# Matrix products that nobody reads, in spare PSUM banks, and newly made engine orders, in a two-layer sequence model on one Trainium2 core

## What is computed

```python
xn = layernorm(x)
# block 1: delta-rule attention (4 heads, dk 128, dv 32) plus two layers of
# local attention (8 heads of 64, window 64) with a gelu feed-forward each
x = x + delta_attention(xn) + local_ffn_depth_2(xn)
xn = layernorm(x)
# block 2: causal attention over a latent of 32 (16 heads of 8)
# plus a mixture of 6 experts (top 2) and one shared expert
x = x + latent_attention(xn) + moe(xn)
```

## Time and profile before

| | |
|---|---|
| time, median of 3 runs | 2025.28 us (2022.1 to 2027.91) |
| the profiled execution's own time | 2022.87 us |
| its span, first to last instruction | 2021.0 us |
| PE busy | 1769.2 us (88%) |
| DVE / ACT / POOL busy | 1351.1 / 927.8 / 818.0 us |
| mean granted TensorE clock | 0.941 |

### The profile page before, as it was taken

One profiled execution on the slowest core, in us unless ns is written; L12 is line 12 of the kernel. 1 busy time (PEld: TensorE's weight loads), 2 busy tenths in 40 slices (PEclk: granted clock), 3 DMA queues, 4 the chain that ended last, 5 costly groups with the idle time before them and its releaser, 6 DMA issues.

```text
span 2021.0 us, 43924 instructions
## 1 busy us (share of the span) xinstructions
PE 1769.2 (88%) x16640; PEld 1142.2 (57%) x16640; DVE 1351.1 (67%) x3602; ACT 927.8 (46%) x2449; POOL 818.0 (40%) x819
## 2 busy tenths in 40 slices
PE   2598669999898989999898989999899989988687
PEld 1375437656584647756575646746475556745343
DVE  3454637777678767787687776687587776575273
ACT  1233425366433745357443754446443754435323
POOL 2344635265145534166144534176144544163000
PEclk9789879999899989999899999999899998999788
DMA  4200112100222012200221012110221011220020
GB/s 177 67 26 12 39 33 62 49 20 23 53 57 58 11 37 77 64 21 12 64 57 49 20 35 71 52 38 10 63 62 49 20 36 31 61 65 4 6 80 6
DMA packets 126625, 89.91 MB, mean 44 GB/s; under 512 B 42168, under 2 KB 113976, under 8 KB 126136
## 3 DMA queue, kind: packets, MB, share of 16 engines
q1 hardware_dynamic: 126128, 86.44, 16.0%
q10 hardware_dynamic: 288, 0.67, 0.1%
HBM read 46.84 MB, written 25.17 MB: 36 GB/s over the span
## 4 chain that ended last, share of the span: by engine, by line
PE 67%; DVE 12%; ACT 8%; issue 6%; POOL 6%; DMA 1%; SPq 0%; DVEq 0%; POOLq 0%; ACTq 0%
PE bank L688 10%; PE bank L1076 4%; PE bank L718 3%; PE bank L795 3%; ACT shared L1322 3%; PE bank L1062 3%; PE bank L775 3%; PE bank L805 3%; PE bank L829 2%; PE bank L1061 2%; PE bank L834 2%; ACT soft L1236 2%; PE bank L1153 2%; PE bank L1034 2%; PE bank L961 2%
## 5 line engine op out<-in xcount | busy, mean ns | idle before, releaser
L1322 ACT ACTIVATE shared<-bank 128x512 f32<-128x512 f32 (+1 forms) x384 | 201.8, 531 | 257.7 <-PE bank L1062 256.4
L1818 POOL TENSOR_TENSOR soft<-soft,prec 128x512 f32<-128x512 f32 x128 | 132.6, 1039 | 441.9 <-DVE prec L1457 441.1
L1626 DVE TENSOR_REDUCE nmx<-bank 128x1 f32<-128x512 f32 (+3 forms) x352 | 223.3, 638 | 98.6 <-PE bank L1034 95.6
L1236 ACT ACTIVATE soft<-bank,nmax 128x128 f32<-128x128 f32 x512 | 179.8, 381 | 121.0 <-DVE nmax L1449 120.3
L1779 POOL TENSOR_TENSOR qk_rs<-qk_rs,minus_half 128x16 f32<-128x16 f32 x64 | 187.5, 2930 | 5.3
L1061 PE MATMUL bank<-b_sb 128*128 128x128 bf16 x512 | 116.8, 229 | 39.7 <-ACT shared L1322 38.6
L1062 PE MATMUL bank<-shared 75*128 75x384 bf16 (+3 forms) x512 | 147.1, 315 | 0.0
L718 PE MATMUL bank<-w_sb,hT 128*128 128x512 f32 x256 | 137.9, 628 | 9.1 <-DVE hT L1396 4.7
L1034 PE MATMUL bank<-shared 72*128 72x256 bf16 (+3 forms) x512 | 126.8, 300 | 0.0
L688 PE MATMUL bank<-c_sb,soft 128*128 128x128 f32 x608 | 99.6, 293 | 25.1 <-POOL soft L1818 14.3
L1076 PE MATMUL bank<-shared,vaug 128*32 128x512 f32 (+3 forms) x1024 | 99.7, 489 | 18.9 <-ACT shared L1322 18.1
(11 more groups left out here) (247 smaller groups left out, 4532.5 us busy)
## 6 DMA issues: line engine op xcount, KB each, us to landing
shared<-parts_dram SPq DMA_DIRECT2D x64, 288.0 KB
vm<-v_f SPq DMA_DIRECT2D x112, 128.0 KB, 2.4
parts_dram<-parts SPq DMA_DIRECT2D x96, 128.0 KB, 2.4
L_dram<-the SPq DMA_DIRECT2D x32, 256.0 KB, 2.4
shared<-X_dram SPq DMA_DIRECT2D x32, 256.0 KB, 3.5
shared<-L_dram SPq DMA_DIRECT2D x32, 256.0 KB, 4.1
w_sb<-weights SPq DMA_DIRECT2D x1, 4167.0 KB, 19.2
x_tm<-x SPq DMA_DIRECT2D x8, 256.0 KB, 3.4
```

The source lines that it names most:

```text
L1236: a = af(v4(p_sb, 2, 4)[:, j, g], place("fS", j)[:, g * P:(g + 1) * P], ACT.Exp, bias=nmax[:, at:at + 1], accum_out=psums[:, at:at + 1])
L1322: af(v4(PTm, 2, GROUP)[:, u % 2, i, 0:n], place("mST", b, i)[:, 0:n], ACT.Exp).then_inc(mexp_done, 1)
L1626: reduce(v3(nmx[:], HM)[:, h:h + len(heads), c], v3(place("mS", b, t)[:, 0:len(heads) * (c + 1) * P], len(heads)), AX, ALU.max, negate=Tru ...
L1818: tt(p, p, spread(prec[:, at:at + NPAIR], P), ALU.mult).then_inc(fnorm_done, 1)
```

## The change

**1. Products that nobody reads.** A step `warm` on PE issues 8 products of the bf16 identity by 128x512 bf16 columns into a bank that is unused at that time. There are 19 such steps, 152 products: 7 in period -1 (behind `hT`, each `fv` and each `k`), 4 in the first layer of period 0 and 4 in its second (each behind an `fS`), and 4 that may stand anywhere ahead of the first `mST` of period 8. The four of the first layer wait for the last `gram` (bank 3), those of the second for `oT0` (bank 0), the last four for the last `fkT` (bank 5). The first `k` of batch 1, which uses bank 3 again, waits for `warm_done`.

**2. All orders anew.** All strings of all five engines and all periods differ, those of periods 1 to 6 and 7 too, in which there is no `warm` step.

```diff
 ORDER = {
     "PE": (
         (
-         "fefeffeefeffefefeeeeee"),
...
+         "feeefeefeefeeffeffeeefeefeffe"),
...
+WARM = 8
...
-            s += [("fS", b, l, c)] + [("fnorm", b, l, c, j) for j in range(2)]
+            s += [("fS", b, l, c)] + ([("warm", "l0" if l == 0 else "l1", WARM)] if b == 0 else []) + [("fnorm", b, l, c, j) for j in range(2)]
...
-    s = []
+    s = [("warm", "end", WARM)] * 4 if b == LAST else []
...
+def warmed(steps, names):
+
+    return [x for step in steps for x in [step] + ([("warm", "start", WARM)] if step[0] in names else [])]
...
-        first = {"f": steps_head(0) + [("hcopy", 0)] + steps_chunks(0, 0, 0, AHEAD), "e": steps_early(0)}
+        first = {"f": warmed(steps_head(0) + [("hcopy", 0)] + steps_chunks(0, 0, 0, AHEAD), ("hT", "fv")), "e": warmed(steps_early(0), ("k",))}
...
+        BANKS = {"warm": lambda site: {"start": 2, "l0": 3, "l1": 0, "end": 5}[site],
...
+                def idle(site, n):
+
+                    if site == "l0":
+                        pe.wait_ge(L_done, NT)
+                    elif site == "l1":
+                        pe.wait_ge(oT0_copied, 1)
+                    elif site == "end":
+                        pe.wait_ge(fkT_copied, ch(BATCH, 0, 0))
+                    for _ in range(n):
+                        m = mm(v3(place("warm", site)[:], 4), B("identb"), repeat(B("identb"), 4), start=True, stop=True, skip_group_check=True)
+                    if site == "l0":
+                        m.then_inc(warm_done, 1)
...
                         if b:
                             pe.wait_ge(oT0_copied, b)
+                        if b == 1:
+                            pe.wait_ge(warm_done, NT)
```

More of the change, by code:

```diff
@@ new lines @@
+         "beffebbbfbffefbefbeebbebebffebfebfbbffbbfbbfffbfbbbbfbbbbbbbbbb"),
+        (
+         "bdmffdbdmdbdfbmddbddffdbddfmdfdbbdbmdbddfmddfdfdbdddmbdbmbddbdfddedfdmddmbddmdddbdbdbdbdmdbddmdbdmbbbbdbbambma"
+         "fafamdfafamfafafafmabamfafabbmbacacfcabcmaccfafcamacbcfacamcabcfbacmcbcafcbacfmcafcabcamccfaeacbbaecabcaecacec"
+         "afbceacbcafccaefaecabebcaefceccaeacbcaeabceccabcafcfccfbcccbccfbbcbccfbccbccbccbccccbc"),
+        (
+         "bdmdffbdbdmbfdmbdfddfddbdfdmfdbdbdbdmbddddfmdffmbdmffdbbdbdbdbdddmbdbmdbdbdmdbddddbdbbbbdbbddbdmmfddddmdfdmdff"
+         "fmafmaadmamfamfafabafmambafmabfabmabmaffacbacmcfacmfabccabcfabcabcfaccabccaffcaacbbccabcaabcabcaccaabcabcabcab"
+         "accbacccacacbcacbcabbababacbabcacbccacccbccccccccccccccccccccccc"),
@@ L67 @@
-        (
-         "bdffdbbddmbdmdddffffdbbfbfbmdmdddfmmmfddbfdbbbddfddddbbmddbbmdddbddfdmfffffmfffmfbbdbcbcffccmffccbcfbcbcbcffcf"
-         "ccbcffcbbcbcccbccbcbcbccccccccbccccccccccccccccccccbcc"),
+         "fdddddfbbbbfddfdddfbdfbbbfffdfddbdfbbddfdbdddbdbdbdbbdddffdddfffdffefefebeebfbbffffeebefebbbfffbffbbffbfffbbbb"
+         "fbffb"),
+        (
+         "bddfbdbfdmdfbdmdddffbfdbddbfbffdfmddbmmbmbdmbdddffdbmdbbbdddddddmdbdffdfmfffffbfmbbcfcbccfcffccmcbcfcbfcbccbfc"
+         "fcfcmcbcfecbbeccbececfccecbecfecfecebcfcbccbcccfccfcccfccbccccfcfcccccb"),
@@ L70 @@
+        (
+         "bfdddbdbfbmdmfdfdfbdfdbfdbdbffddfmmmmbffmdbbdbdbdddbdbddbdmbfddddmdfddffffmfmffdbfbmbbffffccmcbcfbcbcbcffcfccc"
+         "bcfbcbcbcfccbcbcbcbcccccccccbccccccccccccbcccccccccccc"),
         (
-         "mmmmmmmmmmmmccccccccmccccccccccccccccccccccccccccccccccccccccccccc"),),
+         "mmmmmmmmmmmmmccccccccccccccccccccccccccccccccccccccccccccccccccccc"),),
     "DVE": (
         (
-         "ffffeffeeeffeeeeee"),
+         "fffffeeeefefeefeee"),
         (
-         "bddfbbfddefbddbdbdfdbddddddeddbdbddbbddddbddbdddbdbdddddbbddbbddbeddbbbbdfffefeeebbbffebfbbfbeefebebbbfebfbbbf"
@@ new lines @@
+         "bbbbbbbbbbbb"),
+        (
+         "bbmbefmfdddmmmdbmddmbddbmbdfddedbmddfdddmbdmdbbdmmddmdddbddmddmbdbdbddddddmbbmdbdedbmbmbdbdabmbamafafamafafama"
+         "mabababmafaamafambaaambababmafamaffacabambmababaaaeeaeaaebababceabaaffaeaeaaeabbeabafbfbcebbbbbcbc"),
+        (
+         "bmbbfmfmdmddmdbmddbdmbdmbdfddfbdddddmdmmbbmbmdddbbdmbdbmddmddbbddbddbdbddbmdbdbdbdmmfddddmfdmfmafamamamaamafba"
+         "bmamabfamamaabmafbambabafaaabaambaabbaaaabacbababaaaabbabaababacaaabababbababccc"),
@@ L98 @@
         (
-         "feefeefee"),
+         "fefefeeee"),
         (
-         "eddffddfffeefeeefef"),
+         "deddffdfffeeeeeefff"),
         (
-         "eddffdmdmaafffafaeeaeeffeec"),
+         "eddfddmfmafafaffaeeeeaefefc"),
         (
-         "dddmdfmfaffaffaaac"),
+         "ddfmfddmafafffaaac"),
         (
@@ L1175, in e_down @@
                     m.then_inc(ey_psum, 1)
-                walk("PE", {"hT": hT_, "fqk": fqk, "fv": fv, "fqT": fqT, "fkT": fkT, "fS": fS, "fPT": fPT, "fPV": fPV, "fwo": fwo,
+                walk("PE", {"warm": idle, "hT": hT_, "fqk": fqk, "fv": fv, "fqT": fqT, "fkT": fkT, "fS": fS, "fPT": fPT, "fPV": fPV, "fwo": fwo,
                             "fln": fln, "hnT": hnT_, "fg": fg, "fa": fa, "fw2": fw2, "x1": x1, "xn2T": xn2T_,
```

37 lines of the change are left out of this document (11 added, 26 removed).

## The result

The changed kernel takes **2043.6 us** (median of 4, 2041.8 to 2052.6), the kernel before 2023.7 beside it (2020.8 to 2027.9). The ratio is 1.0102, 95% interval 1.0070 to 1.0134. The forecast was 1999 with a range to 2028. It is slower by 20 us, so the sign is wrong as well as the size.

What follows compares the result with a forecast made beforehand. PE was taken to bound the kernel, partly at half clock. Gains of 18 (period ends), 1 (beginning) and 7 (period 0) make 26 us off 2022.87, 1996.9, or 1999 us on the median's footing; range 1973 to 2028.

Steps and rivals of the forecast that it cites:

- Periods 7 and 8 otherwise: Periods 7 and 8 apart from what other terms covered: new order, no sign seen, 0 us, ends -4 and +4.
- the steady end: Period ends, x1 to final, six times: 18.6 us shrinks to about 7.5; net gain 3 us per period, 18 in six.
- The term of the waits: At each period end: 11 us saved, 8.6 given back by moved work and its waits, leaving 2.4 us gained.
- The end of -3 per period: Losing end for each steady period: four new waits of 0.75 us where there were none.
- x1_apply: DVE step near the period's end: takes 1.11 us behind at_tm, making PE wait about 1.2 us.
- The solve that holds up stream b: Rival, middle periods: late blocks stall DVE before solve, up to 7.17 us six times; slower, 2042 us, chance 0.13.
- the other new waits of the middle order: Middle periods: further waits from the new order, given no size, included in the slower rival's chance of 0.13.
- The beginning and period 0: Start: beta at 50, second gram about 1.2 us, net gain 1; period 0: half clock partly returned, gain 7 us.
- The last batch: Period 8: two groups delay latT, two stand where PE idled; net 0 us, ends -5 and +4.
- The price of a group: Eight unread products cost at most 2.4 us at full clock, 4.0 at half; nineteen groups 45 us if nothing hides them.
- The half clock costs little: Rival, whole kernel: without the clock term six ends give 1 us each, the rest 2; 2017 us, sharing a chance of 0.15.
- clock and waits both whole: Rival: full gains, 7 us in each of six period ends and 10 from the start; 1973 us, chance 0.18.

Runs made afterwards that it cites:

- The first run: The changed kernel with period 7's strings on all five engines taken back from the kernel before; 2031.7 us, ratio 1.0027 to the kernel before.
- The second run: The kernel before with only period 7's strings on all five engines taken from the change; 2038.1 us, ratio 1.0057.
- The sixth run: The kernel before with only the strings of periods 1 to 6 taken from the change; 2040.7 us, ratio 1.0064.
- the twelfth run: The changed kernel with DVE's sum of the delta rule (oss) moved behind fw2 in periods 1 to 6; 2060.5 us, ratio 1.0177 to the kernel before.
- The two by two: PE's stretch up to x1 of batch 0 in four kernels: neither orders nor groups 254.8 us, orders alone 264.9, groups alone 263.5, both 251.5.
- the eleventh run: The kernel before plus the change's early strings and 15 groups, small groups at every period end, and four groups in the last batch's old order; 2000.9 us, ratio 0.9895.
- the fourth run: The changed kernel with all 19 groups left out and its new orders kept; 2063.5 us, ratio 1.0173 to the kernel before.

## Why the prediction was wrong

**Where the miss lies.** The sum said 26 us off the span, and 20.9 were added: 46.9 us apart. Period 7 is 20.4 of them. Periods 2 to 6 are 19.5 (15 off forecast at 3 each, 4.5 added). The stretch up to the first `final` is 6.1 (11 off forecast: 1, 7 and 3 for the end of period 1; 4.9 came), the last batch 0.9. So two steps failed, each with some 20 us.

**The first step that failed** is the sentence "Periods 7 and 8 otherwise: the order is new, and I see no sign either way, 0, ends -4 and +4". Period 7 costs 20.4 us, five times its end. Period 7 has its own strings on all five engines, and the working put no price on any row of them. The first run shows that with the old strings the whole loss there is gone, the second that the new ones cost 12.3 us by themselves, 6.6 of it in waits. In the changed kernel the longest wait there is

```profile
1728.40 0.65 PE L1017 MATMUL bank<-shared,U_sb 128*32 128x128 f32 x8 [2.55 <-ACT U_sb L1323]
```

and 14 of the 20 us are lost ahead of the period's end: DVE takes up x1 of batch 7 at 1895.61, 218.3 us into the period, and before at 1881.55, 203.9 us into it. Two windows of PE with the half clock, the first at the wait just shown, the second from x1 to the end:

```profile
1727.00:1735.00 8.00, 6.60 (x48) 0.57 0.24 67
1893.00:1932.00 39.00, 24.86 (x151) 0.62 0.00 1
```

The second run has the same wait of 2.55 us at the same place (ahead of 1728.58), and the full clock around it:

```profile
1727.00:1735.00 8.00, 6.42 (x84) 1.00 0.28 79
```

So the wait alone does not decide whether the half clock comes.

**The second step that failed is the balance of the steady end; its terms were read well.** x1 to `final` takes 7.0 us (forecast 7.5). In period 2 PE is busy 4.5 us less by the clock, in the mean of periods 2 to 6 some 3.4, where I had 2.5. The term of the waits has the wrong sign: I forecast 2.4 less and took off 1.9 for waits that I had no row for, and PE stands still 5.9 more in period 2 and 4.3 more in the mean. "I have no row for what waits arise there" was true, and the gain of 2.4 should then not have been counted. Measured is 0.9 slower per period for 3 faster, 4.5 us in the five. The sixth run shows that the strings do this by themselves: 19 to 20 us of standing still per period for 16 before, and 10 us in the five. The end of -3 per period had allowed for it.

**x1_apply** was taken as 1.2 us of wait behind its 1.11; it takes 2.58 and the wait is 1.94, since POOL's scaling of q and k (L1834) runs beside it. Both in period 2:

```profile
751.24 2.58 DVE L1415 TENSOR_SCALAR soft<-x_tm,mv_f,rs_f 128x128 f32<-128x128 f32 x4
751.18 1.04 POOL L1834 TENSOR_TENSOR q_f<-q_f,qk_rs 128x512 f32<-128x512 f32 x1
```

It is the same pair of engines as in the twelfth run.

**The solve that holds up stream b** did not happen: no wait for the blocks stands in period 2 of the changed kernel, so that rival's mechanism is out, although its 2042 is close to the time that came. Its neighbour, "the other new waits of the middle order", is nearer, and that too missed period 7.

**The beginning and period 0** held in sign and fell short in size. beta comes at 50.74 (forecast 50), the second gram takes 1.16 us (1.2), and these stretches of PE answer to the earlier trace rows:

```profile
110.00:120.00 10.00, 9.68 (x132) 1.00 0.13 39
...
150.00:160.00 10.00, 8.27 (x89) 0.72 0.01 2
```

The long wait is still there, 10.90 us ahead of 90.62 for 12.73. Up to x1 of batch 0 the change gains 3.3 us, for 8 forecast, and up to the first `final` 4.9, for 11. The reason was wrong in part, too. I priced the groups as if the order stood still around them. The two by two shows 8.7 us of loss for the groups alone and 10.1 for the orders alone, and the gain only from the pair.

**The last batch** was put at 0 with ends -5 and +4; it came out 0.9 longer, and the eleventh run shows no gain from its groups either.

**The price of a group** was bounded by 2.4 us at the full clock and is 1.89 in the timeline:

```profile
49.01 1.89 PE L709 MATMUL bank<-b_sb 128*128 128x512 bf16 x8
```

The Trainium skill (TensorE: Matmul & The Clock Gate, "Wait — 56ns, not 53.3ns?") gives 215.7 ns from start to start. By that eight take 1.73 us up to the next start. The trace agrees: the instruction behind this group starts at 50.74, 1.73 us after it.

**"The half clock costs little"** was a rival that the runs refute. The ninth kernel changes no order and adds 176 unread products; its clock is 0.963 instead of 0.941 and it is 0.94% faster, with the first stage as it was. The Trainium skill (TensorE: Matmul & The Clock Gate, "What's actually happening") puts the ramp penalty under 1% of a typical span. Here some 16 of the 19.7 us, 0.8%, came back from the ends of the periods alone, and at 0.963 most of the half clock is still there, so by this estimate the whole is above 1%. But the other end, "clock and waits both whole", would not have been reached by this change either: it assumed that the middle strings gain.

**What stays open.** Why the same strings of period 7 run 8 us longer behind the changed periods than behind the old ones, with the same waits, is measured and not explained. The groups are not the reason: the fourth run has none, and its period 7 lasts 254.8 us with 35.2 of standing still. The twelfth has 250.5 with 35.0. Nor is it known which engine's string in period 7 brings the 6.6 us of waits: the strings of PE, ACT and DVE depend on one another, and mixtures of them were not tried.

## What to carry to other kernels

When a change remakes the order of several stages, price each stage by its own waits; a stage that you have not looked at needs a wide end on the losing side, not a zero with narrow ends. A gain in TensorE's clock is worth only what the order does not take back in waits, so read length less busy beside the clock. Unread products paid here where they filled a wait that was already there and longer than they are (2 products of 0.60 us in a wait of 0.69), and cost more than they returned where they stood in an order made without them (15 groups of 8, 8.7 us in a stretch of 255).

## What had not been expected of the hardware

**DVE and POOL held each other up in some operations.** DVE copies of 64x512 and 64x511 floats took 0.42 us each, and 1.14 and 1.39 where a POOL product of 1.05 and 1.32 us ran at the time. The x1_apply pieces, in the changed kernel beside POOL's scaling, made 2.58 us for four, against 1.11. The copy of 1.39 ended 0.28 us behind the POOL operation beside it (623.76 against 623.48), so it looks like waiting for the whole operation and not like sharing. The Trainium skill (SBUF — State Buffer, "SBUF: two separate sides") calls the port pair that the two share an exclusive lock, which whoever starts first holds for the whole instruction, where the DVE operation is of a kind that uses the pair; these rows agree. So does the other order. In the kernel before, DVE's second copy starts at 629.94, ahead of the same POOL product, and keeps its 0.42, and the product takes 1.21 us instead of 1.05:

```profile
630.06 1.21 POOL L1845 TENSOR_TENSOR shared<-shared,ors 128x512 f32<-128x512 f32 x1
```

The place of one DVE step decides such a meeting: with `oss` behind the copies, it was gone.

**Periods with the same instructions and waits differ by up to 4.6 us through the clock.** In the ninth run PE stands still 11.7 to 11.8 us in each of the periods 2 to 6, and they last 226.3 to 230.9; the granted clock is 1.00 in the shortest and 0.98 in the longest. In the sixth run it is 19 to 20 us, and 230.6 to 233.1. In the kernel before all lie within 0.4. The profile of a kernel can then place a gain or loss of a few us in a period where nothing changed, which is why the totals above were read from medians and the stages only for their size.
